# A gated cross-attention and FP8 feed-forward block on one core: permuted unit matrix for the weights' transposes, mask rows copied by VectorE, another split of the rounding, all engine orders rewritten

## The reference

```python
qp = layernorm(x) @ Wq.T;  k, v = split(ctx @ Wkv_expand.T)      # per head: 32 columns
scores = where(causal, qh @ kh.T / sqrt(32), min)
x = x + tanh(g_xattn) * (softmax(scores) @ vh) @ Wout.T
qx, sx, sc = fp8 of layernorm(x), scaled by row                   # per token
g, u = qx @ fp8(w_gate).T, qx @ fp8(w_up).T                       # 1408 wide, weights scaled by row
t = silu(g) * u
x = x + tanh(g_ffn) * (fp8(t) @ fp8(w_down).T)
```

## Time and profile before

| | |
|---|---|
| median of 3 runs | 734.01 us (732.45 to 735.41) |
| profiled execution, own time | 735.42 us |
| profiled execution, span | 733.7 us |
| PE busy | 664.5 us (91%), granted clock 0.969 on average |
| DVE busy | 664.1 us (91%) |
| ACT busy | 549.0 us (75%) |
| POOL busy | 546.5 us (74%) |
| DMA queue of SP | 148974 packets, 92.68 MB |

### The profile page before, as it was taken

How to read it: one execution, slowest core, us unless ns; L and a number is a source line. 1 busy time by engine, 2 the same in 40 slices (tenths; PEclk the granted TensorE clock), 3 DMA queues, 4 the chain that set the end, 5 groups by cost and what they waited for, 6 DMA issues and landing times.

```text
span 733.7 us, 15607 instructions
## 1 busy us (share of the span) xinstructions
PE 664.5 (91%) x6130; PEld 417.8 (57%) x6130; DVE 664.1 (91%) x1099; ACT 549.0 (75%) x987; POOL 546.5 (74%) x606
## 2 busy tenths in 40 slices
PE   1567889999999999999999999999999999999774
PEld 1456566656666666656565756566666666545331
DVE  5987687999898989999999989999999999899993
ACT  6888768788878796978878787879687868565540
POOL 5777878986868787887878787969597777766551
PEclk9889799999999999999999999999999999999896
DMA  8979875888685749666775757876667664613313
GB/s 308 227 144 201 165 135 99 160 147 158 102 158 92 166 79 195 93 150 110 139 121 136 131 116 143 123 150 112 143 104 147 94 143 76 126 37 78 74 29 96
DMA packets 151207, 95.51 MB, mean 130 GB/s; under 512 B 115326, under 2 KB 121854, under 8 KB 151134
## 3 DMA queue, kind: packets, MB, share of 16 engines
q1 hardware_dynamic: 148974, 92.68, 64.9%
q0 software_dynamic: 576, 1.45, 0.7%
q10 hardware_dynamic: 1584, 0.39, 0.3%
HBM read 31.59 MB, written 9.83 MB: 56 GB/s over the span
## 4 chain that ended last, share of the span: by engine, by line
PE 50%; DVE 24%; ACT 9%; POOL 6%; DMA 5%; issue 2%; SPq 2%; ACTq 0%; POOLq 0%; DVEq 0%
PE pair L1163 30%; PE pair L1401 3%; PE pair L1406 3%; DVE room L2889 3%; PE pair L1432 2%; DVE tm L3240 2%; PE pair L1433 2%; DVE room L3235 2%; POOL PT L799 2%; PE pair L1428 2%; DVE room L2885 2%; DVE mx L3052 2%; DVE room L3278 2%; DVE room L3191 2%; PE pair L1384 1%
## 5 line engine op out<-in xcount | busy, mean ns | idle before, releaser
L835 POOL TENSOR_TENSOR room<-room,up_scale 128x512 f32<-128x512 f32 (+1 forms) x96 | 128.3, 1348 | 38.6 <-ACT room L2303 38.4
L3052 DVE TENSOR_REDUCE mx<-pair 128x6 f32<-128x768 f32 x128 | 116.7, 950 | 4.3 <-PE pair L1339 4.1
L799 POOL TENSOR_SCALAR_AFFINE_SELECT PT<-PT 128x512 f32<-128x512 f32 x128 | 105.6, 854 | 12.4 <-ACT PT L2221 11.7
L2221 ACT ACTIVATE PT<-pair 128x768 f32<-128x768 f32 x128 | 98.0, 816 | 19.3 <-PE pair L1384 16.3
L2303 ACT ACTIVATE room<-room,sx 128x512 f32<-128x512 f32 (+1 forms) x96 | 63.9, 679 | 43.3 <-DVE sx L3156 26.2
L1163 PE MATMUL pair<-WgT,room 128*128 128x512 bf16 (+1 forms) x384 | 91.1, 367 | 4.6 <-DVE room L3235 4.5
L1163 PE MATMUL pair<-WdT,room 128*128 128x512 bf16 x352 | 83.5, 387 | 11.6 <-DMA room<-room 11.6
L1163 PE MATMUL pair<-xT,WqTh 128*128 128x256 bf16 x512 | 88.5, 276 | 4.0 <-ACT x L1979 4.0
L1163 PE MATMUL pair<-WuT,room 128*128 128x512 bf16 (+1 forms) x384 | 91.6, 364 | 0.1
L1163 PE MATMUL pair<-xT,WqTl 128*128 128x256 bf16 x256 | 70.5, 276 | 0.0
L3235 DVE TENSOR_TENSOR room<-pair,room 128x512 f32<-128x512 f32 (+1 forms) x96 | 60.7, 636 | 9.8 <-POOL x L844 6.5
(11 more groups left out here) (137 smaller groups left out, 1854.4 us busy)
## 6 DMA issues: line engine op xcount, KB each, us to landing
xin<-in_x_dram SPq DMA_DIRECT2D x16, 512.0 KB, 4.8
x<-in_x_dram SPq DMA_DIRECT2D x16, 512.0 KB, 3.9
K<-kh SPq DMA_DIRECT2D x32, 256.0 KB, 5.7
Q<-qh SPq DMA_DIRECT2D x32, 256.0 KB, 4.9
out_dram<-x SPq DMA_DIRECT2D x16, 512.0 KB, 3.2
K<-kl SPq DMA_DIRECT2D x16, 256.0 KB, 6.8
Q<-kl SPq DMA_DIRECT2D x16, 256.0 KB, 4.9
room<-in_L_ffn_w_down_dram SPq DMA_DIRECT2D x4, 704.0 KB, 8.0
```

The lines of the kernel that those rows point to most:

```text
L799: pool.affine_select(out=view, in_=view, compare_op=ALU.is_ge, fill=0.0, base=0, pattern=[[0, 2], [0, 2], [1, P]], channel_multiplier=-1). ...
L835: pool.tensor_tensor(g, g, up_scale[:, chunk(n)[1]], ALU.mult).then_inc(slw_done, 1)
L2221: act.activation(head_columns(ring(b, c), 0, 384), head_columns(shifted_pair[c][:, :], 0, 384), ACT.Exp, scale=SCALE).then_inc(exp_done, 1)
L3052: dve.tensor_reduce(mx[:, heads, :], head_columns(w, 0, 3 * P).rearrange("p h (r s) -> p h r s", s=P), AX.X, ALU.max).then_inc(max_done, 1)
```

## The change

1. `attention_weights` transposes with `by_place`, the unit matrix with its columns permuted, for n = 0 and 2 to 5. The transposed piece then stands in PSUM in the heads' order, and copies and subtraction are plain 128x512.
2. The mask rows are built by POOL at partitions 96 to 124 of two 128x128 tiles, `rows_q` and `rows_k`, with the zeros and the -1 of rows 96 to 98 in them. DVE copies them into `Q4[i]` and `K4[i]` (`put_queries`, `put_keys`, four copies of 29x4096 bf16). The DMAs `mask_of_queries`, `mask_of_keys`, `keys_ones` (two each) and `no_maxima(0)`, `no_maxima(1)` go.
3. DVE rounds units 0, 1, 2, 3, 4, 6, 8, 10, 12 and 14, POOL units 5, 7, 9, 11, 13 and 15.
4. All five lists are in a new order, with new waits and new PSUM banks for some products.

```diff
+            rows_q = sb("rows_q", [P, P], BF16)
+            rows_k = sb("rows_k", [P, P], BF16)
...
         def w_views(n, exact=False):
             views = [*w_parts[n], w_exact(n) if exact else bank[aw_bank[n]]]
-            if n == 0 or 2 <= n < 6:
-                views = [v.rearrange("p (g c j) -> p g j c", g=KT, j=G) for v in views[:2]] + \
-                    [views[2].rearrange("p (g j c) -> p g j c", g=KT, j=G)]
             return views
...
+            by_place = ident[:, :].rearrange("p (j c) -> p c j", j=G)
...
-                    last = pe.transpose(bank[aw_bank[n]][:, m * P:(m + 1) * P], src, ident[:, :])
+                    last = pe.transpose(bank[aw_bank[n]][:, m * P:(m + 1) * P], src, ident[:, :] if n == 1 or n >= 6 else by_place)
...
+            def put_queries(i):
+                if i == 0:
+                    dve.wait_ge(const, N_CONST)
+                dve.tensor_copy(Q4[i][96:MASK_END, :, :].rearrange("r h (t s) -> r (h t) s", t=TT),
+                                rows_q[96:MASK_END, None, :].to_broadcast([MASK_END - 96, NH * TT, P])).then_inc(q_put, 1)
...
-            def mask_of_queries(i):
-                if i == 0:
-                    sp.wait_ge(const, N_CONST - 1)
-                sp.dma_start(Q4[i][99:MASK_END, :, :].rearrange("r h (t s) -> r (h t) s", t=TT),
-                             mask_q[:, None, :].to_broadcast([MASK_ROWS, NH * TT, P])).then_inc(mask_q_in[i], 16)
...
-        q_bank = (bank[7], bank[6])
-        v_bank = (bank[7], bank[4])
+        q_bank = (bank[7], bank[3])
+        v_bank = (bank[7], bank[2])
...
-        down_bank = (bank[2], bank[3])
+        down_bank = (bank[4], bank[0])
```

More of the change, by code:

```diff
@@ new lines, in _ @@
+            x_low(4, 1)
+            normalised_low(2, 0)
+            rstd2_made(1)
+            normalised_low(2, 1)
+            keys_low(4, 0)
+            added(0, 0)
+            up_scaled(1, 0)
+            keys_low(4, 1)
+            max_parts(3)
+            up_scaled(1, 1)
+            up_scaled(1, 2)
+            scales1(5)
+            up_scaled(1, 3)
+            up_scaled(1, 4)
+            queries_low(4, 0)
+            causal_part(3, 0)
+            causal_part(3, 1)
+            added(0, 1)
@@ L1569, in _ @@
             shifted(0, 4)
-            unit_turned(9)
+            values(1, 0)
             shifted(0, 5)
@@ L1613, in _ @@
             shifted(1, 7)
+            values(2, 1)
             weighted(1, 1)
-            unit_turned(13)
+            scores(2, 0)
             weighted(1, 2)
             weighted(1, 3)
-            values(2, 1)
+            spread(6)
+            unit_turned(15)
             unit_turned(14)
-            gate_products(0, 0)
-            up_products(0, 0)
-            scores(2, 0)
+            unit_turned(13)
+            keys(3, 0)
+            keys(3, 1)
             scores(2, 1)
@@ L1852, in _ @@
             weighted(13, 3)
-            scores(14, 0)
             values(14, 0)
@@ L1865, in _ @@
             keys(15, 0)
+            keys(15, 1)
             scores(14, 5)
@@ L2302, in silu @@
+                if n == 5 and b == 15:
+                    act.wait_ge(gs_done, 96)
                 g = gs[:, n % 3, 0:width(n)]
@@ new lines, in _ @@
+            silu(1, 1)
+            silu(1, 2)
+            queries_exact(4, 0)
+            abs_t(1, 0)
+            maxima_taken(3)
+            maxima_sent(3)
+            squares1(5, 1)
+            queries_high(4, 1)
+            silu(1, 3)
+            abs_t(1, 1)
+            silu(1, 4)
+            abs_t(1, 2)
+            silu(1, 5)
+            exps(3, 0)
+            exps(3, 1)
+            queries_exact(4, 1)
+            centred(2, 1)
+            exps(3, 2)
+            exps(3, 3)
@@ new lines, in _ @@
+            maxima(2, 0)
+            rounded_x(0, 0)
+            sums_inverted(1)
+            inverse_spread(1, 0)
+            inverse_spread(1, 1)
+            normalised(1, 0)
+            normalised(1, 1)
+            scale_x(0)
+            floored_x(0, 1)
+            maxima(2, 1)
+            lifted_x(0, 1)
+            maxima(2, 2)
+            rounded_x(0, 1)
+            maxima(2, 3)
+            gate(0, 0)
+            residual(1, 0)
+            maxima(2, 4)
+            maxima(2, 5)
@@ new lines, in _ @@
+            maxima(2, 6)
+            gate(0, 1)
+            maxima(2, 7)
+            second_maxima(2)
+            gate(0, 2)
+            up(0, 0)
+            gate(0, 3)
+            up(0, 1)
+            gate(0, 4)
+            up(0, 2)
+            gate(0, 5)
+            largest_t(0, 0)
+            largest_t_inverted(0, 0)
+            floored_t(0, 0)
+            lifted_t(0, 0)
+            residual(1, 1)
+            rounded_t(0, 0)
+            for k in range(1, 9):
+                up(k - 1, 3)
+                largest_x(k, 0)
+                up(k - 1, 4)
@@ new lines, in _ @@
+                maxima(k + 2, 3)
+                residual(k + 1, 0)
+                maxima(k + 2, 4)
+                maxima(k + 2, 5)
+                rounded_x(k, 1)
+                maxima(k + 2, 6)
+                maxima(k + 2, 7)
+                floored_t(k - 1, 1)
+                second_maxima(k + 2)
+                gate(k, 1)
+                up(k, 0)
+                gate(k, 2)
+                lifted_t(k - 1, 1)
+                gate(k, 3)
+                rounded_t(k - 1, 1)
+                up(k, 1)
```

2978 lines of the change are left out of this document (1449 added, 1529 removed).

## The result

The changed kernel takes 741.35 us (median of 5 runs, 739.06 to 742.47), the kernel before 733.37 (5 runs, 732.45 to 735.41). The ratio is 1.0102 with a 95% interval of 1.0076 to 1.0127: **slower by 1%**, where 728.8 us and faster were forecast, and outside the range of 721 to 738. The profiled execution took 742.47 us with a span of 740.7, 7.0 more than that of before.

What follows compares the result with a forecast made beforehand. PE was taken to bound the loop, with VectorE close behind. 4.3 + 1.5 - 1.5 - 0.5 = 3.8 us, plus 1.4, made 5.2 us less: 728.8 us against the median of 734.0, range 721 to 738.

Steps and rivals of the forecast that it cites:

- Loop and end: Loop from about 160 us and end from about 650: new orders and banks, same work; nothing counted, 4 us either way.
- The start: Stretch to about 160 us: input first and plain copies bring first scores 6 us earlier, mT of batch 0 4.3 earlier.
- Plain copies: ACT ahead of the first queries: five copies lose 0.74 us each, 3.7 us in all.
- Copies on VectorE: Four mask-row copies on VectorE in the start: 1.7 us each, 7 us in all; upper bound 4.7 each.
- Rounding: Five roundings moved from POOL to VectorE: 10.6 us less on POOL, 6.1 more on VectorE; loss 1.5 us, 0 to 4.
- Permuted transposes: Twenty f32 transposes in the start reading the unit matrix with a step: 0.5 us lost, at worst 5.3.
- Mask DMAs away, 1.5 us: Loads of units 11 and 10 in the start, no longer with a mask DMA behind: 1.5 us won, 0 to 3.
- Scores ahead of the mark, 1.4 us: Batch 0's scores 6 us earlier, so PE has more done by mT of batch 0: 1.4 us won, 0 to 2.2.
- A new wait in the loop: Rival: PE waits once per batch for a newly shared bank, 0.77 us a batch giving 738 us; chance 0.13.
- VectorE eats the gain: Rival: VectorE's added load in the first 110 us can't be hidden, batch 3 is where it was, 733 us; chance 0.18.
- The new instructions are slow: Rival: copies at 4.7 us, slow transposes and waits for POOL lose 9 us in the start, 738 us; chance 0.09.
- The first rival: Start wins 8 us in place of 4, or a third of the end's waits go: about 721 us; chance 0.10.

Runs made afterwards that it cites:

- the run with part 1 alone: Kernel before plus only the permuted unit matrix for attention-weight transposes, with plain copies and subtractions: 734.17 us against 734.40, ratio 0.9993 (0.9973 to 1.0013).
- The seven runs with edits of the order: Changed kernel with instructions moved in the loop's lists on POOL, ACT, SP, PE or VectorE, singly or combined; ratios against the kernel before from 1.0061 to 1.0290.
- four of five runs: Changed kernel, or it with PE's scores later, with scales, stacked queries or additions moved ahead of other work; all five ratios against the kernel before 1.0150 to 1.0290.
- the fifth (SP's queue): Changed kernel with SP issuing the last stacked queries ahead of the store: 746.85 us, ratio 1.0175 to the kernel before; batches 4 to 12 take 316.1 us.
- first run of the first theory: Changed kernel with POOL's scales1 ahead of the causal cuts and ACT's squares1 ahead of the exponentials: 744.71 us, ratio 1.0150 to the kernel before.
- short ring: Changed kernel with PE's scores later, VectorE's down_scaled and both largest_x earlier, POOL's added(k, 1) ahead of the second cut: 750.17 us, 1.0207 to the kernel before.

## Why the prediction was wrong

**The step that failed** is *Loop and end*: "The same work. ... I count nothing, with 4 us either way." They cost 5.1 + 4.7 + 1.8 = 11.6 us by the marks, 10.6 of them idle time of PE. What the trace shows in its place is, in the loop, a chain that comes around once per batch through POOL, ACT, a DMA, PE and VectorE: batches follow each other every 39.5 us on average (315.81 / 8), where PE has 38.7 us of work (309.54 / 8). The range for this step was three times too narrow, and it had no sign, though I had given its reason: a loop with PE at 40.00 of 40 and VectorE at 37.98 can only lose by a new order.

**The start** went the way that was forecast, and came earlier than forecast. Against mT of batch 0 at 70.3 it came at 68.44, scores at 54.62 against 57 to 58, keys at 22.06 against 26 to 27 (the last `x_low` ends at 18.07, where the walk had 21.3), and mT of batch 4 at 220.31 against "about 220". That the last mark fits so well is in part luck, as the start of the run with part 1 alone shows. The sentence that ended the wrong way is that what the start wins is passed on "as long as the loop behind it stays closed". It did not stay closed.

- *Plain copies*: 0.59 us each, as said. The run with part 1 alone gives it at the end, by its interval, at most 2.0 of the 3.7 us, and by its median 0.2.
- *Copies on VectorE*: mis-sized. I took 1.7 us with a lower bound of 1.7; the changed kernel's timeline shows 1.22, 1.22, 1.22 and 1.85 us, 5.5 in all against 7.
- *Rounding*: VectorE's line of roundings in the feed-forward's form grew from 44.6 to 50.8 us, 6.2 where 6.1 were forecast. From batch 0 to 4 VectorE is busy 9.5 us more (131.80 to 141.31) and PE idle 3.2 us more. Whether the first makes the second was not tested; my 1.5 us for it is of the right kind and perhaps too small.
- *Permuted transposes*: about 0.8 us of PE's time in the run with part 1 alone, where I had 0.5 us and up to 5.3.
- *Mask DMAs away, 1.5 us*: no run tests this term. Batch 0 to 1 takes 36.0 us after the change and 37.6 before, but 35.3 in the run with part 1 alone, which still has these DMAs.
- *Scores ahead of the mark, 1.4 us*: wrong in kind. By the mark of batch 0 PE has had 293 products after the change and 315 before, fewer and not more. By the mark of batch 4 PE has had the same number of products (1730 after, 1729 before), and needed 2.8 us less for them (177.98 against 180.77), at a higher granted clock (0.93 and 0.99 against 0.91 and 0.95). Of the 4.6 us that is the larger part.

**The rivals.** *A new wait in the loop* was the right class, with chance 0.13 and 738 us; the loss per batch of 5.1 / 8 = 0.64 us lies between its 0.43 and 0.74. The tell came true: batch 4 to 15 took 435.3 us, over the 430 named. Its mechanism was wrong. No wait in the loop is for the queries' second half, for the weighted values' bank or for the bank where scores begin. They are for a DMA that stands behind another in SP's order, for POOL's `added`, and for cuts and scales that POOL does one after the other. *VectorE eats the gain* had batch 4 at 224 as its tell, which did not come; but that tell leaned on the traced execution of before, and against the run with part 1 alone the changed kernel loses 4.2 of 5.3 us between batch 0 and batch 4, with VectorE 9.7 us busier (141.31 against 131.60). So this rival is not excluded for the start. *The new instructions are slow* did not come: the copies took 1.22 to 1.85 us in place of its 4.7, and the transposes stayed far from their bound.

**Sums that don't come out.** The first rival's 721 us is reached only if both of its conditions hold: 8 us in place of 4 alone give 728.8 - 4 = 724.8, and a third of the end's 15.1 us alone 723.8. The upper end of the forecast's own range, 733, isn't the sum of the bounds named for it: transposes and VectorE's load at their worst and nothing for the last 1.4 make 728.8 + 4.8 + 2.5 + 1.4 = 737.5. The 4 us of the loop stand in neither. Even so the measured 741.35 lies above all of them.

What stays open is why the ring of the changed order is longer by just this much. The seven runs with edits of the order moved the loop by -3.4 to +9.0 us with the banks as they are, so that the order can set its length is shown; that the new banks have no part in it is only argued, from the lists of waits. One wait there is for a bank, that of `shifted(b, 6)` for VectorE's `up` (1369 in the list, 0.4 us), and these two share a pair in the kernel before too. The 2.6 and 2.8 us of idle time behind batch 12 were not taken apart.

## What to carry to other kernels

When PE is busy 100% in a loop that goes around five engines, its order has found a place where every latency is covered, and a new order is to be priced with a loss per turn, not with nothing: 0.64 us in 8 turns outweighed the 4.6 us of a good start. A wait in the list says where slack ran out, and not yet what to shorten; before moving a step ahead, ask what is then behind it. In the traced loops it won 1.4 us to put free work *into* a wait (0.6 us of VectorE's per batch), and in four of five runs it cost 4 to 11 us, each against the kernel that it was added to, to push work in front of something on the ring; in the fifth (SP's queue) the cost came ahead of the loop. Marks such as mT are to be read with PE's idle time and instruction count beside them, since a new order also moves work across the mark; and a gain in the start of one traced execution is to be held against a second one.

## What the runs showed of the hardware

- A copy of 29 rows by 4096 bf16 elements with a broadcast source took VectorE 1.22 us, less than the 1.7 us that the floor's rate gave, in three of four cases and 1.85 us once. POOL was at work beside all four. In the three, VectorE's copy began first and POOL's instruction beside it took longer (its rounding of 128x1024 3.16 us at 45.24, where 2.12 is usual); in the fourth POOL's rounding had begun first, at 73.92, and the copy at 75.27 was the longer one.
- Turning f32 pieces with the columns of the unit matrix taken in steps of four is slower on TensorE where the plain ones are at their fastest: 397 to 402 ns against 272, and one begins every 0.22 us in place of every 0.11 (runs with part 1 alone and before, eight transposes at about 26 us, granted clock 1.00 in both). At the head of the start the plain ones take 421 ns too, and nothing is lost there. The Trainium skill ("SBUF — State Buffer", on cachelines) has a penalty for accesses that cross to a new 16-byte line each time; the trace agrees with the direction, and the page gives no price.
- ACT's copies that write 128x512 bf16 in steps of four took 1343 ns on average, the plain ones 600.
- POOL's additions take longer beside some of VectorE's work. The second half of `added`, the same instruction each time, takes 1.27 us while VectorE is idle or takes a maximum (first run of the first theory, kernel before), 1.85 beside the last 0.7 us of a rounding (changed kernel), and 2.63 beside a lift of 1.68 us (short ring). In the chain above it is on the ring, 0.6 us each turn, nearly the whole loss per batch. But in the first run of the first theory it took 1.27 us and the loop was slower still, so it is not the cause alone; it was not tested by itself. The Trainium skill ("SBUF — State Buffer", the rules on the shared port pair) has the two engines lock one pair of ports; 1.85 and 2.63 against 1.27 agree with it.
